# Low-rank experts of a four-layer gated decoder: routing by pairs of tiles, ups written ahead of downs

## The chip, the cores and the metric

The kernel runs on one core of a Trainium2 chip. The engines are named as in the profile: PE (TensorE matmuls, with PEld for its weight loads), DVE (VectorE), ACT (ScalarE), POOL (GpSimd) and SP (SyncE, which issues the DMAs). The metric is the device time of one execution, in microseconds (us).

## What is computed

The reference runs 32 sequences of 64 tokens, each token a row of 128 floats, through four layers. Each layer adds a gated attention and then a gated feed-forward to the rows. The change touches one of the eight pieces, the feed-forward of the third layer: every token picks two of four experts, whose weights are one shared matrix plus a low-rank correction of their own.

```python
x = x + jnp.tanh(g_xattn[2]) * _L2_xattn_ref(_layernorm(x), ctx, ctx, mask, ...)
x = x + jnp.tanh(g_ffn[2]) * _L2_ffn_ref(_layernorm(x, axis=-1), Wg, bg, Wi, Wo, A, B)

def _L2_ffn_ref(x, Wg, bg, Wi, Wo, A, B):        # E = 4 experts, F = 512, D = 128
    logits = jnp.einsum('bsd,ed->bse', x, Wg) + bg
    scores = jax.nn.softmax(logits, axis=-1)
    topv, topi = jax.lax.top_k(scores, TOP_K)     # TOP_K = 2
    w = jnp.sum(jax.nn.one_hot(topi, E) * topv[..., None], axis=-2)
    base = jnp.einsum('bsd,fd->bsf', x, Wi)
    lora = jnp.einsum('bser,efr->bsef', jnp.einsum('bsd,erd->bser', x, A), B)
    h = jax.nn.relu(base[:, :, None, :] + lora)
    expert_out = jnp.einsum('bsef,df->bsed', h, Wo)
    return jnp.einsum('bse,bsed->bsd', w, expert_out)
```

## The kernel before

The 2048 rows are worked in four blocks of 512 rows. A block is four tiles of 128 rows, which lie on the partitions; tiles 0 and 1 are the first pair, tiles 2 and 3 the second. Each block passes eight stages one after the other (`ffn0`, `attention`, `ffn1`, `attention`, `ffn2`, `perceiver`, `attention`, `ffn3`), so a stage runs four times in the kernel. All of it is written by hand: each engine has its own list of instructions, in the order of the code, and waits on semaphores. An engine never passes over an instruction that waits. There is no scheduler, and no data moves by DMA in the stages spoken of here.

The work touched is `ffn2`. The matrix `w_f2e` holds, for each expert, the shared matrix plus its correction, made once at the start. All matmuls are in float32, each recorded as two passes, so four 128x512 matmuls show as eight instructions.

The stage in front of it is an `attention` (turn 3). It ends with a normalisation of the rows on DVE: pair 0 is normalised while its last two tiles are still on their way, pair 1 after them. Each pair takes bn_stats, bn_aggr, a variance, a root that POOL computes (L267), and a scaling (L292) that writes `xn`.

`ffn2` before, engine by engine:

- PE runs `turn_pairs` (L349): three 128x512 matmuls of constants, `keep_clock` (L347), whose results nobody reads, then the transposes of pair 0 and pair 1 (L361). Then come the router for all four tiles (L1254), the four 128x512 ups (L1263) of tile 0 and of tile 1, and from there, per tile, `turn`: four transposes (L1271) of the summed experts and four matmuls (L1278), the down. The next tile's ups follow it.
- ACT copies the transposed rows (L377), takes the exponentials of the routing (L1294) and waits for the routing weights of all tiles, `comb_ready`. Then it runs, per tile and expert, a relu of the ups scaled by the expert's weight (L1303), and per tile a copy of the transposed sum (L1309).
- DVE does the routing of all four tiles: logits (L1321), the best eight (L384), the places of the best two (L387, L388), one-hots (L394 to L396), the softmax's sum and division (L1330 to L1333). Then it adds the four experts of a tile (L1340, L1343, L1345), adds the down to `x` (L1348), and after tiles 1 and 3 normalises a pair for the next stage.
- POOL computes two roots of the next stage's normalisation.

An up needs its bank free (a relu four ups earlier), a `turn` needs the sum, a down the copy. After it comes `perceiver`. Its PE list begins with the transposes of pair 0 (L367), then two 128x512 matmuls each of the keys (L1422), the queries (L1406) and the values (L1415), and the transposes of pair 1. ACT, DVE and POOL work from those.

## Time and profile before

| | us |
|---|---|
| median of three runs | 1601.91 |
| lowest and highest of the three | 1597.54, 1604.3 |
| the profiled execution | 1598.2 |
| its span, from first to last instruction | 1596.4 |
| mean granted TensorE clock of the span | 0.964 of full speed |
| stage `ffn2` in blocks 0, 1 and 2, by windows | 29.7 each |
| stage `ffn2` in block 3 | 31.9 |

The profile is one execution, and its times are counted from the span's start. A row of the timeline is an instruction or a run of like ones: start, duration, engine, line, operation, output and inputs, count, and in brackets how long the engine had been idle before it and what released it. A granted clock of 1.00 is the full 2.4 GHz, 0.50 is 1.2 GHz, and a value between is a window that holds some of each.

### The profile page before, as it was taken

To read this page: it belongs to the slowest core of one execution; us is meant where nothing else is said; L and a number is where in the kernel's file an instruction comes from. 1 tells how busy PE (TensorE), PEld (TensorE's weight loads), DVE (VectorE), ACT (ScalarE), POOL (GpSimd) and SP (SyncE) were. 2 spreads that over 40 slices of the span, in tenths; PEclk is the share of its full clock that TensorE was granted. 3 is DMA by queue.
4 is the path that set the end of the run, shared out by engine and by line. 5 is a ranking of instruction groups with operands and counts; after the bars stand their busy time and mean duration, and the time that the engine had idled before them with its cause. 6 is when DMAs were issued, how large, how long until landed. Compare 5 with 4: busy or idle time off the path is not lost.

```text
span 1596.4 us, 28486 instructions
## 1 busy us (share of the span) xinstructions
PE 1356.1 (85%) x10940; PEld 896.8 (56%) x10940; DVE 1086.4 (68%) x3253; ACT 746.2 (47%) x1406; POOL 362.1 (23%) x302
## 2 busy tenths in 40 slices
PE   4788987897987998798898899889788799888977
PEld 4455744564654664466465575446556467445745
DVE  3456975877656796686764687687755669658774
ACT  0144544763334643575324553467433455257632
POOL 1131310540131220251014031054013212015300
PEclk8799999999999999999899999999999999899999
DMA  9000000000000000000000000000000000000000
GB/s 355 2 1 1 1 1 1 1 1 17 1 7 1 1 1 1 1 1 16 3 1 7 1 1 1 1 1 2 17 1 7 1 1 1 1 1 2 1 1 7
DMA packets 15094, 18.95 MB, mean 12 GB/s; under 512 B 2776, under 2 KB 13672, under 8 KB 14444
## 3 DMA queue, kind: packets, MB, share of 16 engines
q1 hardware_dynamic: 14960, 17.13, 3.1%
q8 instruction: 88, 1.44, 0.4%
q14 instruction: 46, 0.38, 0.1%
HBM read 16.08 MB, written 1.05 MB: 11 GB/s over the span
## 4 chain that ended last, share of the span: by engine, by line
PE 58%; DVE 24%; ACT 7%; issue 6%; POOL 2%; DVEq 0%; POOLq 0%; ACTq 0%
PE bank L1034 7%; PE bank L1045 5%; PE bank L1422 4%; PE bank L1427 4%; PE bank L846 3%; PE bank L1263 3%; DVE work L640 2%; DVE small L646 2%; PE bank L1833 2%; PE bank L1815 2%; PE bank L870 2%; PE bank L1415 2%; DVE small L639 2%; PE bank L1458 2%; PE bank L347 2%
## 5 line engine op out<-in xcount | busy, mean ns | idle before, releaser
L267 POOL TENSOR_TENSOR root<-variance,minus_half 128x2 f32<-128x2 f32 (+1 forms) x72 | 55.3, 768 | 691.5 <-DVE variance L284 421.1
L1087 ACT ACTIVATE work<-bank,w_f 128x512 f32<-128x512 f32 x128 | 88.0, 688 | 90.4 <-PE bank L1034 90.1
L1045 PEld LDWEIGHTS bank<-w_f1d,work 128*128 128x128 f32 x1024 | 119.1, 192 | 13.4 <-issue 13.4
L1045 PE MATMUL bank<-w_f1d,work 128*128 128x129 f32 x1024 | 119.9, 275 | 0.0
L1034 PE MATMUL bank<-xnT,w_f 128*128 128x512 f32 x256 | 118.5, 608 | 0.0
L1596 ACT ACTIVATE work<-work,small 128x128 f32<-128x128 f32 x256 | 78.5, 390 | 84.8 <-DVE small L1723 84.8
L1654 POOL TENSOR_TENSOR small<-small 128x16 f32<-128x16 f32 x32 | 92.9, 2904 | 106.5 <-DVE small L1682 104.9
L639 DVE TENSOR_REDUCE small<-bank 128x8 f32<-128x512 f32 x96 | 65.6, 684 | 32.6 <-PE bank L506 32.6
L1681 DVE TENSOR_REDUCE small<-work 128x16 f32<-128x1024 f32 x48 | 58.4, 1217 | 40.3 <-ACT work L1560 38.7
L521 PE MATMUL bank<-consts,work 128*128 128x128 f32 x384 | 58.9, 291 | 27.9 <-ACT work L605 27.3
L1422 PE MATMUL bank<-w_x,cxT 128*128 128x512 f32 x128 | 62.3, 608 | 21.9 <-DVE work L1695 17.1
L1427 PEld LDWEIGHTS bank<-consts,work 128*128 128x128 f32 x576 | 64.3, 140 | 29.2 <-issue 16.8
L521 PEld LDWEIGHTS bank<-consts,work 128*128 128x128 f32 x384 | 42.3, 145 | 66.5 <-ACT work L605 42.4
L1427 PE MATMUL bank<-consts,work 128*128 128x128 f32 x576 | 74.8, 275 | 5.2 <-DVE work L1695 2.3
L956 DVE TENSOR_TENSOR work<-bank,work 128x256 f32<-128x256 f32 x64 | 27.2, 425 | 76.1 <-POOL work L921 73.8
L1119 POOL TENSOR_TENSOR small<-small,minus_half 128x4 f32<-128x4 f32 x32 | 42.9, 1340 | 150.1 <-DVE small L1173 150.1
L870 PEld LDWEIGHTS bank<-w_l,work 128*128 128x128 f32 x352 | 53.0, 199 | 40.0 <-ACT work L902 31.8
L1034 PEld LDWEIGHTS bank<-xnT,w_f 128*128 128x128 f32 x256 | 47.1, 193 | 48.9 <-issue 48.9
L846 PE MATMUL bank<-w_l,xnT 128*128 128x512 f32 x128 | 73.2, 662 | 0.0
L605 ACT ACTIVATE work<-work 128x512 f32<-128x512 f32 x96 | 59.4, 632 | 28.3 <-DVE work L640 28.2
L612 ACT COPY work<-bank 128x512 f32<-128x512 f32 x96 | 53.0, 585 | 40.0 <-PE bank L521 40.0
L377 ACT COPY xnT<-bank 128x256 f32<-128x256 f32 x32 | 11.2, 374 | 126.1 <-PE bank L361 126.1
(284 smaller groups left out, 3211.5 us busy)
## 6 DMA issues: line engine op xcount, KB each, us to landing
w_f<-in_f_dram SPq DMA_DIRECT2D x1, 2616.0 KB
w_f<-in_f_dram SPq DMA_DIRECT2D x1, 2180.0 KB, 26.5
w_x<-in_x_dram SPq DMA_DIRECT2D x1, 2115.0 KB
w_l<-in_l_dram SPq DMA_DIRECT2D x1, 2088.5 KB, 20.7
w_f1d<-in_f1d_dram SPq DMA_DIRECT2D x4, 512.0 KB
work<-in_x_dram SPq DMA_DIRECT2D x4, 256.0 KB, 2.9
work<-in_ctx_dram SPq DMA_DIRECT2D x4, 256.0 KB, 3.3
out_dram<-x SPq DMA_DIRECT2D x4, 256.0 KB, 2.3
```

Of the source, the lines that this page charges most:

```text
L521: m = pe.transpose(banks[4 + half][:, (c % 4) * P:(c % 4 + 1) * P], p_sb[t % 2][:, c * P:(c + 1) * P], ident)
L605: act.activation(p_sb[t % 2][:, own], s_sb[t % 2][:, own], ACT.Exp).then_inc(p_ready, 1)
L639: link(dve.tensor_reduce(mx[:, t, hs], s, AX, ALU.max))
L846: m = pe.matmul(a[:, :], xt, k_l0["gu"][:, g * 512:(g + 1) * 512], start=True, stop=True)
L870: m = pe.matmul(banks[6 + t % 2][:, 0:D], hidT[s % 2][:, c * P:(c + 1) * P], k_l0["down"][:, (2 * g + c) * D:(2 * g + c + 1) * D], start=( ...
L1034: pe.matmul(banks[n % 3][:, :], k_f1["w1"][:, e * 512 + c * P:e * 512 + (c + 1) * P], xnT[:, :], start=True, stop=True).then_inc(up_done, 1)
L1045: pe.matmul(z_of(e, t)[:, 0:129], hT[e % 2][:, c, t * P:(t + 1) * P], w_f1d[:, c, e, :], start=(c == 0), stop=(c == 3))
L1087: act.activation(hT[e % 2][:, c, :], banks[n % 3][:, :], ACT.Relu, bias=k_f1["b1"][:, n:n + 1]).then_inc(hT_ready, 1)
L1422: pe.matmul(banks[j][:, :], cxT[:, b, :, :], half_of(k_x3["wkv"], j), start=True, stop=True).then_inc(k_done, 1)
L1427: m = pe.transpose(bank[:, (c % 4) * P:(c % 4 + 1) * P], rows[:, c * P:(c + 1) * P], ident)
L1596: ins = act.activation(s_sb[b % 2][:, c * P:(c + 1) * P], s_sb[b % 2][:, c * P:(c + 1) * P], ACT.Exp, bias=negmax[b % 2][:, c:c + 1])
L1654: pool.tensor_tensor(k_rs, k_ssq, half_power, ALU.pow).then_inc(k_rooted, 1)
```

## The change

Only `ffn2` and the table of fill matmuls change.

- The three fill matmuls ahead of the stage's rows go.
- PE transposes pair 0, routes it and computes two ups of tile 0 before it transposes pair 1; the second pair's router stands between the ups of tile 0. The transposes go to banks 4 and 5.
- The routing on DVE is done for two tiles at a time. The first pair's is run whole; the second's is cut in three and laid between the adds of tile 0.
- The relus of tile 0 have the scale 1.0 and don't wait for the routing. DVE multiplies the weights in while it adds: one multiplication (L1378) and three multiply-adds (L1382) take the place of three adds.
- The ups of tile t+2 now stand behind the transposes of tile t and ahead of its down.

```diff
@@ -35,7 +35,7 @@
-FILL_BEFORE_ROWS = (0, 0, 0, 2, 3, 0, 0, 3)
+FILL_BEFORE_ROWS = (0, 0, 0, 2, 0, 0, 0, 3)
@@ -1247,16 +1250,15 @@
-                    turn_pairs(pe, prev, turn_no, xn)
-                    wait_for(pe, prev.all_used)
-                    pe.wait_ge(rowsT_ready, due(rowsT_ready, 2 * turn_no + 2))
...
-                    m.then_inc(routed, 1)
-
-                    def up(t):
...
+                    def route(pair):
+                        pe.wait_ge(rowsT_ready, due(rowsT_ready, 2 * turn_no + pair + 1))
+                        for t in pair_tiles(pair):
+                            m = pe.matmul(banks[6 + pair][:, t * 4:(t + 1) * 4], xnT[:, t * P:(t + 1) * P], k_f2["wg"],
+                                          start=True, stop=True)
+                        m.then_inc(routed, 1)
+
+                    def up(t, experts):
+                        for e in experts:
                             n = 4 * t + e
                             if n >= 4:
                                 pe.wait_ge(r_ready, due(r_ready, n - 3))
...
                             m = pe.transpose(banks[4 + t % 2][:, c * P:(c + 1) * P], r[t % 2][0][:, c * P:(c + 1) * P],
                                              ident)
                         m.then_inc(turned, 1)
+
+                    def down(t):
                         pe.wait_ge(gT_ready, due(gT_ready, t + 1))
+                        pe.wait_ge(comb_ready, due(comb_ready, t % 2 + 1))
...
@@ -1279,34 +1284,56 @@
-                    for t in range(TILES + 1):
-                        if t < TILES:
-                            up(t)
-                        if t == 0:
-                            pe.wait_ge(comb_ready, due(comb_ready, 1))
-                        if t >= 1:
-                            turn(t - 1)
+                    turn_pair(pe, turn_no, xn, 0, banks[4])
+                    wait_for(pe, prev.all_used)
+                    route(0)
+                    up(0, (0, 1))
+                    turn_pair(pe, turn_no, xn, 1, banks[5])
+                    up(0, (2,))
+                    route(1)
+                    up(0, (3,))
+                    up(1, range(4))
+                    for t in range(TILES):
+                        turn(t)
+                        if t + 2 < TILES:
+                            up(t + 2, range(4))
+                        down(t)
 
-                    take_pairs(act, turn_no)
-                    act.wait_ge(shifted, due(shifted, 1))
-                    act.activation(ex, shifted_lg, ACT.Exp).then_inc(exp_ready, 1)
+                    def relus(t, experts):
+                        for e in experts:
+                            act.wait_ge(up_done, due(up_done, 4 * t + e + 1))
+                            if t >= 2 and e == 0:
+                                act.wait_ge(turned, due(turned, t - 1))
+                            weight = 1.0 if t == 0 else comb[:, t, e:e + 1]
+                            act.activation(r[t % 2][e], banks[e][:, :], ACT.Relu, scale=weight).then_inc(r_ready, 1)
+
+                    def exps(pair):
...
+                        own = slice(2 * pair, 2 * pair + 2)
+                        act.wait_ge(shifted, due(shifted, pair + 1))
+                        act.activation(ex[:, own, :], shifted_lg[:, own, :], ACT.Exp).then_inc(exp_ready, 1)
+
+                    def take(t):
...
+                        act.copy(gT[t % 2], banks[4 + t % 2][:, :]).then_inc(gT_ready, 1)
+
+                    take_pair(act, turn_no, 0, banks[4])
+                    relus(0, (0, 1))
+                    take_pair(act, turn_no, 1, banks[5])
+                    exps(0)
+                    relus(0, (2, 3))
                     act.wait_ge(comb_ready, due(comb_ready, 1))
-                    for t in range(TILES + 1):
-                        if t < TILES:
-                            for e in range(4):
-                                act.wait_ge(up_done, due(up_done, 4 * t + e + 1))
-                                if t >= 2 and e == 0:
-                                    act.wait_ge(turned, due(turned, t - 1))
-
-                                act.activation(r[t % 2][e], banks[e][:, :], ACT.Relu,
-                                               scale=comb[:, t, e:e + 1]).then_inc(r_ready, 1)
-                        if t >= 1:
-                            act.wait_ge(turned, due(turned, t))
-                            if t >= 3:
-                                act.wait_ge(down_done, due(down_done, t - 2))
-                            act.copy(gT[(t - 1) % 2], banks[4 + (t - 1) % 2][:, :]).then_inc(gT_ready, 1)
+                    relus(1, (0, 1))
+                    exps(1)
+                    relus(1, (2, 3))
+                    for t in range(TILES):
+                        take(t)
+                        if t + 2 < TILES:
+                            act.wait_ge(comb_ready, due(comb_ready, 2))
+                            relus(t + 2, range(4))
 
@@ -1317,32 +1344,59 @@
-                    dve.wait_ge(routed, due(routed, 1))
...
+
+                    def routing(pair):
+                        own, pw = slice(2 * pair, 2 * pair + 2), [P, 2, 4]
+                        dve.wait_ge(routed, due(routed, pair + 1))
+                        logits = banks[6 + pair][:, 8 * pair:8 * pair + 8].rearrange("p (t e) -> p t e", t=2)
+                        link(dve.tensor_tensor(lg[:, own, 0:4], logits,
+                                               k_f2["bg"].unsqueeze(1).to_broadcast(pw), ALU.add))
+                        link.last_of([dve.max(best[:, t, :], lg[:, t, :]) for t in pair_tiles(pair)])
+                        dve.tensor_tensor(shifted_lg[:, own, :], lg[:, own, 0:4], best[:, own, 0:1].to_broadcast(pw),
                                           ALU.subtract).then_inc(shifted, 1)
-
-                    best, place = top_two(dve, link, lg, 8, 160, with_best=shift)
-                    dve.wait_ge(exp_ready, due(exp_ready, 1))
...
+                        yield
+                        link.last_of([dve.max_index(where[:, t, :], best[:, t, :], lg[:, t, :]) for t in pair_tiles(pair)])
+                        link(dve.tensor_copy(place[:, own, :], where[:, own, 0:2]))
+                        iota = k_const["iota"][:, 0:4].unsqueeze(1).to_broadcast(pw)
+                        link.last_of([dve.tensor_tensor(one, iota, place[:, own, k:k + 1].to_broadcast(pw), ALU.is_equal)
+                                      for k, one in enumerate((comb[:, own, :], tmp[:, own, :]))])
+                        link(dve.tensor_tensor(comb[:, own, :], comb[:, own, :], tmp[:, own, :], ALU.add))
+                        yield
+                        dve.wait_ge(exp_ready, due(exp_ready, pair + 1))
+                        link(dve.tensor_reduce(den[:, own, 0], ex[:, own, :], AX, ALU.add))
+                        link(dve.reciprocal(den[:, own, :], den[:, own, :]))
+                        link(dve.tensor_tensor(ex[:, own, :], ex[:, own, :], den[:, own, :].to_broadcast(pw), ALU.mult))
+                        link(dve.tensor_tensor(comb[:, own, :], comb[:, own, :], ex[:, own, :], ALU.mult))
+                        dve.sem_inc(comb_ready, 1)
+                        yield
+                    def add_experts(t, steps):
+
+                        acc = r[t % 2][0]
+                        dve.wait_ge(r_ready, due(r_ready, 4 * t + 2))
+                        if t == 0:
+                            link(dve.tensor_scalar(acc, acc, comb[:, t, 0:1], None, ALU.mult))
+                        for e in (1, 2, 3):
+                            dve.wait_ge(r_ready, due(r_ready, 4 * t + e + 1))
+                            if t == 0:
+                                ins = dve.scalar_tensor_tensor(acc, r[t % 2][e], comb[:, t, e:e + 1], acc, ALU.mult, ALU.add)
+                            else:
+                                ins = dve.tensor_tensor(acc, acc, r[t % 2][e], ALU.add)
+                            if e == 3:
+                                ins.then_inc(sum_ready, 1)
+                            else:
+                                link(ins)
+                                some(steps, 1)
+
+                    run(routing(0))
+                    second = routing(1)
                     next_rows = iter(())
                     for t in range(TILES + 1):
                         some(next_rows, 3)
                         if t < TILES:
-                            dve.wait_ge(r_ready, due(r_ready, 4 * t + 2))
-                            link(dve.tensor_tensor(r[t % 2][0], r[t % 2][0], r[t % 2][1], ALU.add))
-                            some(next_rows, 1)
-                            dve.wait_ge(r_ready, due(r_ready, 4 * t + 3))
...
+                            add_experts(t, next_rows if t else second)
+                        if t == 0:
+                            run(second)
                         if t >= 1:
```

On PE, from the last project of the attention to the second down, the list before was:

```order
L547 MATMUL bank<-w_x,small 128x128
L347 MATMUL bank<-w_x,consts 128x512 x3
L361 MATMUL bank<-consts,xn 128x128 x4
L1254 MATMUL bank<-w_f,xnT 128x4 x4
L1263 MATMUL bank<-w_f2e,xnT 128x512 x8
L1271 MATMUL bank<-consts,work 128x128 x4
L1278 MATMUL bank<-w_f,work 128x128 x4
L1263 MATMUL bank<-w_f2e,xnT 128x512 x4
L1271 MATMUL bank<-consts,work 128x128 x4
L1278 MATMUL bank<-w_f,work 128x128 x4
```

The same stretch of PE's list now (L1256 is the router, L1265 the ups, L1273 the transposes, L1283 the downs):

```order
L547 MATMUL bank<-w_x,small 128x128
L367 MATMUL bank<-consts,xn 128x128 x2
L1256 MATMUL bank<-w_f,xnT 128x4 x2
L1265 MATMUL bank<-w_f2e,xnT 128x512 x2
L367 MATMUL bank<-consts,xn 128x128 x2
L1265 MATMUL bank<-w_f2e,xnT 128x512
L1256 MATMUL bank<-w_f,xnT 128x4 x2
L1265 MATMUL bank<-w_f2e,xnT 128x512 x5
L1273 MATMUL bank<-consts,work 128x128 x4
L1265 MATMUL bank<-w_f2e,xnT 128x512 x4
L1283 MATMUL bank<-w_f,work 128x128 x4
L1273 MATMUL bank<-consts,work 128x128 x4
```

Three matmuls left the front, four ups moved from behind each of the first two downs to the front of it.

At the end of the stage, PE's list up to the first transposes of the perceiver (L367), before and now:

```order
L1263 MATMUL bank<-w_f2e,xnT 128x512 x4
L1271 MATMUL bank<-consts,work 128x128 x4
L1278 MATMUL bank<-w_f,work 128x128 x4
L1271 MATMUL bank<-consts,work 128x128 x4
L1278 MATMUL bank<-w_f,work 128x128 x4
L367 MATMUL bank<-consts,xn 128x128 x2
```

```order
L1265 MATMUL bank<-w_f2e,xnT 128x512 x4
L1283 MATMUL bank<-w_f,work 128x128 x4
L1273 MATMUL bank<-consts,work 128x128 x4
L1283 MATMUL bank<-w_f,work 128x128 x4
L1273 MATMUL bank<-consts,work 128x128 x4
L1283 MATMUL bank<-w_f,work 128x128 x4
L367 MATMUL bank<-consts,xn 128x128 x2
```

The last four ups now stand ahead of three downs, where they stood ahead of two.

On DVE, from the first routing's end to the first tile's sum, now (the three pieces of the second routing lie between the multiply-adds):

```order
L1369 TENSOR_TENSOR small<-small 128x8
L1378 TENSOR_SCALAR work<-work,small 128x512
L1382 SCALAR_TENSOR_TENSOR work<-work,small 128x512
L1352 TENSOR_TENSOR small<-bank,w_f 128x2x4
L1354 MAX small<-small 128x8 x2
L1355 TENSOR_TENSOR small<-small 128x8
L1382 SCALAR_TENSOR_TENSOR work<-work,small 128x512
L1358 MAX_INDEX small<-small 128x8 x2
L1359 CAST small<-small 128x4
L1361 TENSOR_TENSOR small<-consts,small 128x8 x2
L1363 TENSOR_TENSOR small<-small 128x8
L1382 SCALAR_TENSOR_TENSOR work<-work,small 128x512
```

Before, three adds (L1340, L1343, L1345) stood in this place behind the whole routing.

## Rows read from the trace of the kernel before

**Rows 1.** The page, part 4: shares of the chain that ended last.

```profile
PE 58%; DVE 24%; ACT 7%; issue 6%; POOL 2%; DVEq 0%; POOLq 0%; ACTq 0%
```

**Rows 2.** Chain that ended last, block 0's stage: start, length, what.

```profile
246.79 0.61 DVE xn L292 x2
...
252.36 0.18 DVE small L1333
252.63 0.70 ACT work L1303
253.32 0.14 issue
253.46 3.69 PE bank L1263 x8
```

**Rows 3.** Windows over the stage, blocks 0, 3: width, PE, PEld, DVE, ACT, POOL busy, PEclk.

```profile
243.60:273.30 29.70, 25.00 (x100) 14.00 (x101) 16.28 (x57) 13.43 (x23) 1.39 (x2) 1.00 0.00 0
1392.30:1424.20 31.90, 27.71 (x100) 15.22 (x101) 16.08 (x57) 13.33 (x23) 1.39 (x2) 0.91 0.00 1
```

**Rows 4.** Timeline of block 0, PE in the stage.

```profile
244.09 2.74 PE L347 MATMUL bank<-w_x,consts 128*128 128x512 f32 x6
...
256.97 0.60 PE L1271 MATMUL bank<-consts,work 128*128 128x128 f32 x4
...
258.38 1.16 PE L1278 MATMUL bank<-w_f,work 128*128 128x128 f32 x8 [0.82 <-ACT work L1309]
...
259.38 3.60 PE L1263 MATMUL bank<-w_f2e,xnT 128*128 128x512 f32 x8
...
273.34 0.38 PE L367 MATMUL bank<-consts,xn 128*128 128x128 f32 x2
```

**Rows 5.** Timeline of block 0, DVE at the routing.

```profile
247.58 0.09 DVE L1319 MEMSET small<- 128x32 f32 x1 [0.18 <-DVE xn L292]
...
249.64 0.17 DVE L1321 TENSOR_TENSOR small<-bank,w_f 128x16 f32<-128x16 f32 x1 [1.97 <-PE bank L1254]
249.85 0.37 DVE L384 MAX8 small<-small 128x8 f32<-128x8 f32 x4
...
250.35 0.09 DVE L387 MATCH_VALUE_LOAD small<-small 128x8 f32 x1
...
251.02 0.17 DVE L388 CAST small<-small 128x8 f32<-128x8 uint32 x1
```

**Rows 6.** Groups by line and form, DVE: busy and mean ns of one.

```profile
L1189 DVE SCALAR_TENSOR_TENSOR x<-work,small,x 128x128 f32<-128x128 f32 x128 | 36.8, 347 | 1.2 <-DVE small L1186 0.2
...
L1170 DVE TENSOR_SCALAR work<-work 128x512 f32<-128x512 f32 x32 | 13.7, 427 | 1.1
...
L1340 DVE TENSOR_TENSOR work<-work 128x512 f32<-128x512 f32 x16 | 11.1, 692 | 18.7 <-ACT work L1303 18.7
...
L762 DVE SCALAR_TENSOR_TENSOR work<-bank,tg,xn_next 128x512 f32<-128x512 f32 x4 | 3.0, 745 | 0.0
```

**Rows 7.** Timeline of block 0, DVE and POOL at the stage's end.

```profile
265.43 0.35 DVE L1348 SCALAR_TENSOR_TENSOR x<-bank,tg,x 128x128 f32<-128x128 f32 x1 [0.93 <-PE bank L1278]
...
266.62 0.17 DVE L282 TENSOR_SCALAR variance<-norm_small 128x2 f32<-128x2 f32 x1
266.86 0.70 POOL L267 TENSOR_TENSOR root<-variance,minus_half 128x2 f32<-128x2 f32 x1 [20.11 <-DVE variance L282]
```

**Rows 8.** Timeline, PE, at gaps of other stages.

```profile
384.13 0.76 PE L521 MATMUL bank<-consts,work 128*128 128x128 f32 x4 [2.40 <-ACT work L605]
...
1535.04 1.12 PE L521 MATMUL bank<-consts,work 128*128 128x128 f32 x4 [2.40 <-ACT work L605]
```

**Rows 9.** Windows around falls of the clock; columns as in Rows 3.

```profile
384.00:388.00 4.00, 3.30 (x56) 2.58 (x56) 3.28 (x6) 2.58 (x6) 0.00 (x0) 0.57 0.01 2
1534.00:1542.00 8.00, 6.75 (x69) 3.99 (x70) 6.11 (x10) 3.37 (x6) 0.00 (x0) 0.57 0.01 3
1391.00:1399.00 8.00, 6.43 (x12) 2.99 (x12) 3.96 (x14) 0.38 (x2) 1.14 (x2) 0.57 0.00 0
```

**Rows 10.** Timeline, PE at half clock, blocks 3 and 0.

```profile
1392.95 5.33 PE L347 MATMUL bank<-w_x,consts 128*128 128x512 f32 x6
...
385.45 1.11 PE L521 MATMUL bank<-consts,work 128*128 128x128 f32 x4 [0.56 <-ACT work L605]
```

**Rows 11.** Chain that ended last, block 0, into the perceiver.

```profile
274.93 1.96 PE bank L1422 x4
276.88 0.87 PE bank L1406 x2
277.78 0.60 ACT work L1569
```

25 lines of the change are left out of this document (7 added, 18 removed).

## The prediction

> **What bounds the kernel now.** I read the shares of the chain first: PE holds 58% of it and DVE 24% [rows 1], so what counts in a stage is who hands work to PE. Then the same chain inside the changed stage [rows 2]. It runs from the second pair's normalised rows (246.79, ready at 247.40) over transposes, router and the whole routing on DVE to the first relu at 252.63, and only that relu frees the bank for the next ups at 253.46. From there the stage is a loop of transposes, copy, down and four ups. The windows say how long the stage is: 29.7 us in block 0 and alike in blocks 1 and 2, 31.9 us in block 3, where the granted clock was 0.91 [rows 3]. The stage is 7.6% of the span, so even a tenth of it is 12 us in four blocks.
>
> The profiled execution took 1598.2 us, 1.8 us more than its span. I make the sum against it and carry the difference over to the median of 1601.9, which lies 3.7 us higher.
>
> **Head of the stage: from the second pair's rows to the first tile's transposes.** Before, the transposes L1271 began at 256.97 [rows 4], 9.57 us after the rows at 247.40. In the new order PE works ahead on pair 0 (rows ready at 244.3): its transposes, two routers and two ups end at about 247.6, the six other ups, the second pair's transposes and routers at 253.7, with 0.86 us an up (3.60 us for four and a bit of overlap [rows 4]). ACT follows each up by about a microsecond. DVE becomes what decides, since it can't start to route before the second pair is normalised. Its list, start to start:
> - memset and first routing. For four tiles the routing took 2.88 us from 249.64 to the end of L1333 at 252.53 [rows 2, 5]. With two tiles the four MAX8 (0.37) halve, and the four searches (250.35 to 251.02, 0.67) halve; the other ten steps read so few elements that they keep their time. That gives 2.88 - 0.19 - 0.33, some 2.4, plus 0.13 for the memset from 247.58: ready at 250.2.
> - the multiplication L1378, 128x512 with one scalar per partition. The trace has it with constants, 427 ns [rows 6]; with a scalar that is read I take 0.48, bounds 0.43 and 0.75. With its semaphore 0.52.
> - three multiply-adds L1382: 745 ns each for the same shape [rows 6], 0.78 with the semaphore, 2.34. The adds that they replace took 692.
> - the first two pieces of the second routing, which lie between them: 0.6 and 1.1, the parts of the 2.4 above.
> 250.2 + 0.52 + 2.34 + 1.7 is 254.8, so the transposes start at 254.85, 2.1 us earlier. PE is done with its ups at 253.7 and has 1.2 us of slack there; ACT, with the last relu of tile 0 at about 251.1, has more. The removed fills cost nothing before in blocks 0 to 2: they ran from 244.09 to 246.83 [rows 4], and pair 1 was ready only at 247.40.
>
> **Middle and end: from the first transposes to the perceiver.** Before: 256.97 to 273.34, 16.37 us [rows 4]. Now transposes 0.5, ups 3.44, down 0.96, transposes 0.5, ups 3.44: the second down starts at 263.7, and PE never waits, since the copy (0.6) and the sums lie under the ups. That part is the gain of ups in front of downs, some 0.9 us for each copy that PE waited for. But DVE takes the second down into x only 1.2 us after it starts (258.38 to 259.58 before), at 264.9, and nothing of its list may pass that. Behind it stand the next normalisation's first steps (265.43 to 266.8 before, 1.4 us [rows 7]), an add of 0.72, the two scalings at 0.6, and two adds: the last tile's sum is ready at 269.2. PE has nothing to do from the end of the third down at 266.9 until then, a gap of 2.35 us. Last transposes 269.3, copy 0.64, down 270.6, and the perceiver's transposes start at 271.6: 16.7 us, 0.3 longer than before. What the new order won in the middle, DVE's order takes back at the end.
>
> Net with the clock held: 2.1 - 0.3 = 1.8 us a block, for PE's and DVE's ends alike, **-7.1 us** in four blocks.
>
> **Block 3.** There the clock fell ahead of the stage and the three fills took 5.33 us [rows 10] where they take 2.74; pair 1's transposes came 2.3 us later than its rows allowed. Without fills that is gone, and the ups at half clock stay inside the slack of 1.2 us and DVE's list. **-2.3 us.**
>
> **The clock at the end of the stage.** PE's clock was 1.00 through the whole stage in three blocks [rows 3]. The new gap of 2.35 us stands behind transposes and a down, and is followed by 0.6 us of transposes, another 0.67 us of waiting, a down and 1.2 us for the perceiver's first copy. The nearest rows are the gaps of 2.40 us ahead of L521 in the third attention [rows 8]: there are four, one a block (384.13, 765.83, 1148.13, 1535.04), and the clock fell at each of them, between 0.2 us before the gap's end and 1.0 us after it. It then stood at half for 3.4 us (three of the four; a 4 us window at 0.57) or for 6.9 us (8 us windows at 0.57 [rows 9]), as it did at 1391, where PE had little to do in the fall's first half. I expect the fall here in all four blocks. Its price: a 128x512 pass costs 0.43 us more at half clock (5.33 against 2.74 for six [rows 10]), and four 128x128 transposes 0.5 more (1.11 [rows 10] against 0.60 [rows 4]). The perceiver's start is on the chain [rows 11]: eight passes of keys and queries and four of values, from 273.1. A spell of 6.9 us that begins between 268 and 271.5 reaches 275 to 278, so it takes in two to five and a half of these passes, 0.9 to 2.4 us, and some part of the last transposes and down, 0 to 1.3 us. I take 2.1; the bounds are 0.5 (a short spell) and 3.6. **+8.4 us**, 2.0 to 14.4.
>
> The Trainium skill speaks against the change here: TensorE: Matmul & The Clock Gate, Part 4: PE-mode transpose, says that transposes don't count as PE being busy in the way that matmuls do, and two of the three things that PE does between 264.7 and 273 are transposes. By that rule the fall would be sure in all four blocks; the trace can't separate it, since the gaps of rows 8 fell without it.
>
> **Sum:** -7.1 - 2.3 + 8.4 = -1.0: 1597.2 us for the profiled execution, **1600.9 us** against the median. With the bounds of the fall alone, 1594.5 to 1607.
>
> **Rivals.**
> - The clock holds at the end, or falls so late that it is back before the perceiver's matmuls. For it speaks that the head of the stage has gaps of 1.4 us with little between them and fell in one block of four. Against it, the four falls out of four at 2.40 us. Then -9.4: 1592.5 us.
> - Slower: the fills were what held the clock at the head. If they go, PE does only short work from 238 to 245.8 and the clock falls there in all blocks, for 6.9 us as at 1391 [rows 9]. The ups from 245.8 to 252.3 then pass at half, 7.5 passes instead of 15: 3.2 us lost, less PE's slack of 1.2, 2.0 a block, on top of the fall at the end. It decides from the third block on. 1600.9 + 8 = 1609 us, 1611 with the far bound of the spell. Against it: at 1391 the clock fell in spite of the fills to come.
> - The change doesn't do what it says: DVE's list is as long as before. With L1378 at 0.75, and halves of the routing that take as long as the whole, the first transposes come 0.9 us earlier, not 2.1, and the sum is +4: 1605 us.
> - Multiply-adds from SBUF at half rate. The rows speak against it: L1189 with both tensors in SBUF takes 347 ns [rows 6], L1348 with one in PSUM 0.35 us [rows 7]. From 128 to 512 columns the time grows by 0.40, so a doubled stream costs 0.53 more each, 1.6 a block, 6.4 in all: 1607 us. This is what the Trainium skill would have, Vector Engine (DVE) Microarchitecture Reference, 7. Points that are easy to get wrong: this instruction with two SBUF sources that aren't bf16 runs at half throughput. The trace does not agree.
>
> **Chances.** Clock falls at the end, about no change: 0.50. Clock holds: 0.27. Falls at the head too: 0.10. DVE's list no shorter: 0.08. Multiply-adds at half rate: 0.05. About 0.5%, 8 us, is what a measurement of this kernel can tell from no change, so faster is under 1593.9 and slower over 1609.9. The held clock lies at the first edge and gives most of faster, with a small part of the forecast's: 0.28. Slower: the head's fall and the far ends of two others: 0.14. Same: 0.58. The range goes from 1591, under which lies a quarter of the held clock's case, to 1607, over which lie the head's fall and some of the last two.
>
> **What the new profile would show.** The first transposes of the stage (L1273) some 7.5 us after pair 1's rows, where it was 9.6; the perceiver's transposes 16.7 us behind them; a gap of PE of about 2.35 us ahead of the last L1273, released by DVE's last add; a granted clock under 0.9 in the windows of the perceiver's first 5 us in three or four blocks, and 1.00 at the ups. L1382 at 745 ns and L1378 at 480. Wrong would be a clock of 1.00 through the perceiver's start, ups at half clock, or a first sum that waits for ACT's relus.

## The result and the profile after

| | before | after |
|---|---|---|
| median, us (runs) | 1600.07 (4) | 1617.24 (4) |
| range, us | 1597.54 to 1604.3 | 1615.41 to 1621.38 |
| profiled execution, us | 1598.2 | 1615.41 |
| its span, us | 1596.4 | 1613.6 |
| mean granted clock | 0.964 | 0.940 |

The changed kernel takes 1.0102 of the time before, interval 1.0081 to 1.0123: 16 us slower. The forecast was no change, and 1617 lies ten microseconds over its range.

The chain's shares are those of [rows 1], but for a point of ACT. The page's own strip (before, then after) of the granted clock, 40 slices in tenths, already says where to look: it is under 9 in ten slices, where before's is in four, and the mean over the span fell by 0.024.

```profile
PEclk8799999999999999999899999999999999899999
...
PEclk8799987999999999899999998889999999989989
...
PE 58%; DVE 24%; issue 6%; ACT 6%; POOL 2%; DVEq 0%; POOLq 0%; ACTq 0%
```

I cut each block in three at instructions that both kernels have: the **head**, from the last L547 of the attention to the first transposes of the stage; the **tail**, from there to the perceiver's first transposes L367; and the **start** of the perceiver, to its second L367. Microseconds, blocks 0 to 3, from the timelines of the two:

| | before | after |
|---|---|---|
| head | 13.21, 13.21, 13.21, 15.50 | 12.97, 11.02, 12.98, 11.01 |
| tail | 16.37, 16.37, 16.38, 16.38 | 18.29 in all four |
| start | 6.82 in all four | 9.03, 8.87, 9.06, 8.90 |

Heads are 7.2 us less in sum, tails 7.7 more, starts 8.6 more. The two profiles are single executions, and they part before the change does anything: block 0's last L547 stands at 243.76 before and at 245.20 after, since the clock had fallen at other places in the two by then. So 1.4 us of the 17.2 between the spans aren't the change's.

PE's timeline of the kernel after, tail of block 0 (start, length, line, what; in brackets the wait and its releaser), answers [rows 4]:

```profile
267.76 0.60 PE L1273 MATMUL bank<-consts,work 128*128 128x128 f32 x4
269.03 1.16 PE L1283 MATMUL bank<-w_f,work 128*128 128x128 f32 x8 [0.68 <-ACT work L1321]
272.80 1.12 PE L1273 MATMUL bank<-consts,work 128*128 128x128 f32 x4 [2.61 <-DVE work L1384]
274.59 2.08 PE L1283 MATMUL bank<-w_f,work 128*128 128x128 f32 x8 [0.68 <-ACT work L1321]
276.46 0.63 PE L367 MATMUL bank<-consts,xn 128*128 128x128 f32 x2
278.30 3.75 PE L1476 MATMUL bank<-w_x,cxT 128*128 128x512 f32 x4 [1.20 <-ACT cxT L1606]
```

The gap of 2.61 us is there, released by DVE's last add. Everything behind it takes twice its time: transposes 1.12 for 0.60, a down 2.08 for 1.16, and the perceiver's four passes 3.75 where [rows 11] has 1.96. The windows show the clock (width, busy of PE, PEld, DVE, ACT, POOL, granted clock, DMA), block 0 ahead of, in and behind the spell (a stretch at half clock), then blocks 1 to 3 in it:

```profile
268.00:272.00 4.00, 1.51 (x12) 1.08 (x10) 3.11 (x10) 0.58 (x1) 1.08 (x1) 1.00 0.00 0
272.00:282.00 10.00, 7.32 (x19) 4.49 (x20) 2.81 (x10) 2.20 (x4) 0.69 (x1) 0.50 0.00 0
282.00:286.00 4.00, 3.87 (x11) 1.59 (x9) 2.64 (x4) 2.74 (x6) 0.00 (x0) 0.97 0.00 0
657.00:668.00 11.00, 7.29 (x19) 4.46 (x20) 3.71 (x12) 2.20 (x4) 0.69 (x1) 0.53 0.00 0
1046.80:1057.00 10.20, 7.56 (x19) 4.67 (x20) 2.81 (x10) 2.35 (x5) 0.69 (x1) 0.50 0.00 0
1432.40:1442.80 10.40, 7.31 (x19) 4.47 (x20) 3.13 (x11) 2.20 (x4) 0.69 (x1) 0.51 0.00 0
```

The clock fell in all four blocks, as forecast, from 2.4 to 1.2 GHz; in block 0 it fell inside the gap, at 272.0, and came back at 282.3, after 10.2 us, where I had taken 6.9. The releaser of the gap is DVE's list, block 0, which answers [rows 7]:

```profile
267.96 0.35 DVE L1402 SCALAR_TENSOR_TENSOR x<-bank,tg,x 128x128 f32<-128x128 f32 x1 [2.37 <-PE bank L1283]
268.34 0.49 DVE L275 BATCH_NORM_STATS2 bn_small<-x 128x6 f32<-128x128 f32 x2
...
269.39 1.08 POOL L267 TENSOR_TENSOR root<-variance,minus_half 128x2 f32<-128x2 f32 x1 [21.21 <-DVE variance L282]
270.58 0.60 DVE L292 TENSOR_SCALAR xn<-x,norm_small,root 128x128 f32<-128x128 f32 x2 [0.66 <-POOL root L267]
271.21 1.53 DVE L1384 TENSOR_TENSOR work<-work 128x512 f32<-128x512 f32 x2
```

DVE takes x, normalises, and only then makes the two adds that PE waits for. POOL's root, beside an add of DVE, took 1.08 us; in [rows 7] it takes 0.70.

**The head.** The heads come in two kinds, 11.0 and 13.0. Windows of the ups in block 0 (long; block 2 reads the same) and block 1 (short), and block 0 around the fall:

```profile
245.00:252.00 7.00, 6.25 (x15) 3.53 (x16) 4.28 (x25) 1.32 (x3) 0.69 (x1) 0.53 0.00 1
633.00:644.00 11.00, 9.28 (x30) 4.36 (x30) 8.96 (x45) 5.98 (x12) 0.69 (x1) 1.00 0.01 1
244.20:244.70 0.50, 0.00 (x0) 0.00 (x0) 0.50 (x1) 0.00 (x0) 0.07 (x1) 1.00 0.00 0
244.70:245.20 0.50, 0.00 (x1) 0.01 (x1) 0.47 (x3) 0.00 (x0) 0.00 (x0) 0.52 0.00 0
```

```profile
245.20 0.80 PE L547 MATMUL bank<-w_x,small 128*128 128x128 f32 x2 [1.40 <-DVE small L647]
```

The long heads are those in which the clock fell before the ups. It fell at 244.7, half a microsecond ahead of the last L547, which already takes 0.80 us for the 0.49 that it takes at full clock; in block 2 it fell at 1019.5, ahead of the L547 at 1019.96. The removed fills would have stood behind this L547, so they could not have held the clock in these two heads. In the short one of block 1, PE's and DVE's steps answer the sum of the prediction: the second pair's rows are ready at 636.80 and the first transposes start 7.40 us later, and PE has waited 1.11 us for DVE's last multiply-add.

```profile
636.20 0.60 DVE L292 TENSOR_SCALAR xn<-x,norm_small,root 128x128 f32<-128x128 f32 x2 [0.81 <-POOL root L267]
...
639.66 0.48 DVE L1378 TENSOR_SCALAR work<-work,small 128x512 f32<-128x512 f32 x1
...
644.20 0.65 PE L1273 MATMUL bank<-consts,work 128*128 128x128 f32 x4 [1.11 <-DVE work L1382]
```

### The profile page after: what moved, and what is told of

It is laid out like the page before. It is cut to its first block, busy times and chain, and to the rows that moved or that the text cites. A ratio compares the mean times of both kernels' runs of the same rounds, so it can differ in the third digit from the quotient of the medians.

```text
span 1613.6 us, 28506 instructions
## 1 busy us (share of the span) xinstructions
PE 1374.0 (85%) x10916; PEld 912.1 (57%) x10916; DVE 1093.3 (68%) x3297; ACT 746.9 (46%) x1410; POOL 363.3 (23%) x302
## 4 chain that ended last, share of the span: by engine, by line
PE 58%; DVE 24%; issue 6%; ACT 6%; POOL 2%; DVEq 0%; POOLq 0%; ACTq 0%
PE bank L1034 7%; PE bank L1045 5%; PE bank L1476 4%; PE bank L1481 4%; PE bank L846 3%; PE bank L347 2%; PE bank L1265 2%; DVE work L640 2%; DVE small L646 2%; PE bank L1887 2%; PE bank L1869 2%; PE bank L870 2%; PE bank L1469 2%; DVE small L639 2%; PE bank L1512 2%
## 5 line engine op out<-in xcount | busy, mean ns | idle before, releaser
L267 POOL TENSOR_TENSOR root<-variance,minus_half 128x2 f32<-128x2 f32 (+1 forms) x72 | 56.7, 788 | 698.4 <-DVE variance L284 427.9
L1476 PE MATMUL bank<-w_x,cxT 128*128 128x512 f32 x128 | 69.5, 668 | 21.9 <-DVE work L1749 17.1
L640 DVE TENSOR_TENSOR work<-bank,small 128x512 f32<-128x512 f32 x96 | 66.4, 691 | 3.3
```

The source lines that it names most:

```text
L640: ins = dve.tensor_tensor(d, s, mx[:, t, hs].unsqueeze(2).to_broadcast([P, 8, SEQ]), ALU.subtract)
L1476: pe.matmul(banks[j][:, :], cxT[:, b, :, :], half_of(k_x3["wkv"], j), start=True, stop=True).then_inc(k_done, 1)
```

## The experiments

**Theory A:** the gap of 2.6 us ahead of the last transposes lets the clock fall, and this alone costs more than the head wins; what is left is a gain. **Rival B:** the new order is slow in itself (DVE's longer list, relus from SBUF, two routings), and the clock is a side effect. **Rival C:** what is lost is lost because everything behind moved in time, so that the clock falls at other places; any shift would do the same. A further question was what the removed fills had been worth.

The results, each against the kernel before on the same chip; heads, tails and starts in us for blocks 0 to 3 as above:

| run | ratio (interval) | head | tail | start |
|---|---|---|---|---|
| e1_fill_tail_gap | 0.9986 (0.9969, 1.0002) | 12.99, 12.81, 12.98, 11.03 | 16.90, 16.96 x3 | 6.82 x4 |
| e3_downs_first | 0.9957 (0.9936, 0.9979) | 11.03, 12.98 x3 | 16.29 to 16.37 | 6.81 x4 |
| e4_ups_first_alone | 1.0079 (1.0053, 1.0105) | 13.20 x3, 14.04 | 17.65, 17.64, 17.65, 17.23 | 9.94, 10.06, 8.59, 9.07 |
| e2_before_no_head_fills | 1.0053 (1.0034, 1.0073) | 15.83, 15.97, 16.19, 15.21 | 16.38 x4 | 6.82 x4 |
| e6_sum_before_norm | 0.9881 (0.9846, 0.9916) | 11.02, 11.03, 12.92, 12.93 | 14.75 to 14.82 | 6.85, 8.54, 6.84, 6.85 |
| e7_downs_first_attention_fill | 0.9941 (0.9921, 0.9960) | 11.03 x4 | 17.98, 16.30, 17.98, 16.29 | 6.82 x4 |
| e10_exps_ahead | 0.9971 (0.9955, 0.9986) | 11.02, 12.98, 12.91, 12.84 | 16.3 to 16.4 | 6.81 x4 |
| e8_sum_first_and_fill | 0.9930 (0.9909, 0.9952) | 11.04, 11.38, 11.03, 11.84 | 14.82 x4 | 6.85 x4 |
| e5_before_shifted | 1.0061 (1.0041, 1.0081) | 13.34, 14.03, 13.21, 14.26 | 16.38 x4 | 6.82 x2, 8.51, 6.82 |
| e12_before_shifted_less | 1.0048 (1.0029, 1.0068) | 15.50, 13.20 x3 | 16.38 x4 | 6.82, 6.81, 8.51, 6.81 |
| e11_after_shifted | 1.0153 (1.0132, 1.0174) | 12.80, 11.02, 11.03, 12.94 | 18.29 x3, 17.77 | 8.90, 8.94, 8.80, 8.58 |
| e13_after_shifted_less | 1.0146 (1.0118, 1.0174) | 12.82, 11.03, 12.93, 12.99 | 18.28, 18.29, 17.77, 17.76 | 8.93, 8.80, 8.58, 8.62 |

### The gap filled

The kernel after with four passes on PE (whose result nobody reads) ahead of the last transposes:

```diff
                     for t in range(TILES):
+                        if t == TILES - 1:
+                            pe.wait_ge(r_ready, due(r_ready, 14))
+                            keep_clock(pe, banks[1], 2)
                         turn(t)
```

> The changed kernel with two matmuls of constants (four passes, about 1.7 us) ahead of the last tile's transposes, where PE waits 2.6 us for DVE. Theory A, the gap lets the clock fall: the clock stays at 1.00, the last transposes to the perceiver take 16.7 us instead of 18.3 from the first ones, the perceiver's start 6.8 instead of 8.9, and some more behind it comes back too, 4 to 5 us a block in all: 1597 to 1602 us against 1617 of the changed kernel. Theory B, the fall has nothing to do with the gap (missing fills at the head, or the transposes): the clock still falls and the time stays at 1614 to 1620.

Median 1600.83 us. PE's timeline of this kernel, block 0, and the windows over tail and start of the four blocks:

```profile
267.64 1.88 PE L347 MATMUL bank<-w_x,consts 128*128 128x512 f32 x4
...
270.42 0.66 PE L1273 MATMUL bank<-consts,work 128*128 128x128 f32 x4 [0.89 <-DVE work L1387]
```

```profile
266.00:283.00 17.00, 12.38 (x44) 6.29 (x44) 10.61 (x35) 7.04 (x13) 4.08 (x6) 1.00 0.00 0
651.00:668.00 17.00, 12.48 (x44) 6.28 (x44) 10.26 (x34) 6.91 (x14) 4.41 (x6) 1.00 0.00 0
1036.00:1053.00 17.00, 12.35 (x46) 6.28 (x44) 10.58 (x36) 7.03 (x13) 3.94 (x6) 1.00 0.00 0
1419.00:1436.00 17.00, 12.48 (x44) 6.28 (x44) 10.61 (x34) 6.92 (x14) 4.36 (x6) 1.00 0.00 0
```

DVE's list and all waits for it are as they were; only the clock differs, 1.00 in all four blocks. Tails fall from 18.29 to 16.96 and starts from 8.97 to 6.82: 14 us in four blocks, of the 1.16% (18 us) that the two ratios differ by. That is theory A's; B can't explain it. The gain that A promised besides is hardly there (the interval reaches 1), since here the clock fell at the head in three blocks. The other 4 us lie outside of tail and start and aren't shown to be the gap's.

### Downs before ups, and ups before downs alone

The kernel after, with the down back in front of the ups of the next tile but one:

```diff
                         turn(t)
+                        down(t)
                         if t + 2 < TILES:
                             up(t + 2, range(4))
-                        down(t)
```

> The changed kernel with the downs ahead of the ups again, as before; head, routing by pairs and relus stay changed. Theory A: last gap gone, tail 16.4 us and perceiver's start 6.8, the head keeps its 2.2 us where the clock is held there: 1596 to 1602 us. Theory B: no more than the 0.3 us a block that the order itself costs comes back: 1614 to 1619 us.

Median 1593.72 us. PE's timeline of this kernel, block 0: the last transposes wait for nobody, and the window over tail and start stands at 1.00 (as it does in the other three blocks).

```profile
266.77 0.60 PE L1273 MATMUL bank<-consts,work 128*128 128x128 f32 x4
268.18 1.16 PE L1283 MATMUL bank<-w_f,work 128*128 128x128 f32 x8 [0.82 <-ACT work L1321]
269.18 0.60 PE L1273 MATMUL bank<-consts,work 128*128 128x128 f32 x4
```

```profile
265.00:282.00 17.00, 12.91 (x49) 6.71 (x47) 10.22 (x30) 9.29 (x18) 3.98 (x6) 1.00 0.00 0
```

With everything else of the change kept, this is 0.4% under before (a difference of the size that a mere shift can make, as shown below), and the tail is no longer than before's. So what made the change slower is one edit of the five, ups in front of downs. The reverse puts that edit alone into the kernel before:

```diff
-                    for t in range(TILES + 1):
-                        if t < TILES:
-                            up(t)
-                        if t == 0:
-                            pe.wait_ge(comb_ready, due(comb_ready, 1))
-                        if t >= 1:
-                            turn(t - 1)
+                    up(0)
+                    pe.wait_ge(comb_ready, due(comb_ready, 1))
+                    up(1)
+                    for t in range(TILES):
+                        turn(t)
+                        if t + 2 < TILES:
+                            up(t + 2)
+                        down(t)
```

> The kernel before with only the ups put ahead of the downs; fills, routing and relus as before. Theory A: the clock falls at the end of the stage in all four blocks, 1.9 us in the tail, 2.2 in the perceiver's start and about 1 behind it: 1616 to 1621 us. Theory B (the head is the cause): 1599 to 1603 us.

Median 1615.24 us. Its timeline, block 0, and the windows over tail and start, blocks 0 and 3 (in block 1 the spell is as long as in block 0, in block 2 as in block 3):

```profile
273.44 0.66 PE L1271 MATMUL bank<-consts,work 128*128 128x128 f32 x4 [2.49 <-DVE work L1348]
```

```profile
270.00:287.00 17.00, 12.59 (x36) 6.84 (x35) 7.44 (x19) 4.95 (x10) 1.76 (x2) 0.70 0.00 0
...
1432.00:1449.00 17.00, 11.51 (x36) 6.34 (x36) 8.37 (x24) 5.89 (x12) 1.76 (x2) 0.80 0.00 0
```

The same gap (2.49 us), the same four falls, 0.8% lost: this edit alone is enough. Adding it and removing it point to the same cause from both sides.

### The sum before the normalisation

If DVE's order makes the gap, DVE's order can close it. The kernel after, where the sum of a tile is finished before any step of the next normalisation:

```diff
                     for t in range(TILES + 1):
-                        some(next_rows, 3)
                         if t < TILES:
-                            add_experts(t, next_rows if t else second)
+                            add_experts(t, iter(()) if t else second)
                         if t == 0:
                             run(second)
+                        run(next_rows)
```

> The changed kernel with one thing moved on DVE: the last tile's three adds come ahead of the next stage's normalisation steps instead of behind and between them. PE's order stays ups first. Theory A: the last gap shrinks from 2.6 to about 0.6 us, so the clock holds and the tail takes 15 us instead of 18.3 and the perceiver's start 6.8 instead of 8.9: 1588 to 1597 us. Theory B (ups first costs in itself, whatever the gap): 1608 us or more.

Median 1583.39 us against 1601.11: 0.9881, under the range that was expected. DVE, POOL and PE of this kernel, block 0:

```profile
267.65 2.15 DVE L1384 TENSOR_TENSOR work<-work 128x512 f32<-128x512 f32 x3
...
269.86 0.66 PE L1273 MATMUL bank<-consts,work 128*128 128x128 f32 x4 [0.36 <-DVE work L1384]
...
270.76 0.70 POOL L267 TENSOR_TENSOR root<-variance,minus_half 128x2 f32<-128x2 f32 x1 [21.32 <-DVE variance L282]
...
272.30 0.41 PE L367 MATMUL bank<-consts,xn 128*128 128x128 f32 x2
```

The gap goes from 2.61 to 0.36 us, the normalisation is still done before PE wants it at 272.30, and the tail is 14.8 us, 1.6 less than before. The gain of ups in front of downs, which the prediction put at some 0.9 us for each copy and saw taken back by DVE, is real once DVE's order lets it through. This kernel is faster than the one before and the changed one.

### The head: what the fills were worth

The kernel before with its three fills at the head taken out, one number:

```diff
-FILL_BEFORE_ROWS = (0, 0, 0, 2, 3, 0, 0, 3)
+FILL_BEFORE_ROWS = (0, 0, 0, 2, 0, 0, 0, 3)
```

> The kernel before without the three matmuls of constants ahead of the stage, nothing else. Theory A: they matter only at the head; the block that lost 2.3 us through slow fills gains it, another may lose up to 3 us by ups at half clock: 1597 to 1606 us. Theory B, the missing fills are what costs the 17 us: 1612 us or more.

Median 1611.41 against 1602.82: it lies between the two ranges. That is 8.6 us, and the longer heads of the profiled execution make up 8.1 of them. PE's timeline of this kernel, block 0, and the window at its head:

```profile
244.49 0.49 PE L547 MATMUL bank<-w_x,small 128*128 128x128 f32 x2 [1.40 <-DVE small L647]
...
248.23 0.69 PE L361 MATMUL bank<-consts,xn 128*128 128x128 f32 x2 [2.62 <-DVEq L307]
...
251.18 9.31 PE L1263 MATMUL bank<-w_f2e,xnT 128*128 128x512 f32 x16
```

```profile
244.00:251.00 7.00, 3.17 (x14) 2.34 (x14) 3.11 (x14) 0.74 (x2) 0.69 (x1) 0.60 0.00 0
```

The fills that I had costed at nothing held the clock in this order of PE: without them it falls at 245.4, where they would have run, and the heads of blocks 0 to 2 grow by 2.6 to 3.0 us. In block 3, where it fell ahead of the last L547 with the fills and without, the head shrinks by 0.3.

So there are two kinds of falls at a head, and only one of them is the fills'. I read where each began, by windows, in all traces without the attention's fill that comes next. With the three fills (before, e4, e5, e12) the clock fell in 5 heads of 16, each time 0.4 to 0.9 us ahead of the last L547 and never behind it. Without them (after, e1, e2, e3, e6, e10, e11, e13) it fell in 22 of 32: in 8 ahead of it as before, in 14 some 0.9 to 1.6 us behind it, where fills would have run. Both falls in the profile of the kernel after are of the first kind.

Would the head be short in all blocks if PE had some work in the attention's end? The kernel with downs first, and two passes more there:

```diff
+                        if turn_no == 3 and step == TILES + 2:
+                            wait_for(pe, (s_ready, 6))
+                            keep_clock(pe, banks[1], 1)
                         if 0 <= step - 3 < TILES:
...
                         turn(t)
+                        down(t)
                         if t + 2 < TILES:
                             up(t + 2, range(4))
-                        down(t)
```

> The kernel with the changed head and the downs first, and one matmul of constants (two passes) put into PE's wait ahead of the last project of the attention in front of the stage, where PE idles 1.4 us. Theory A for the head: it holds the clock there, so the stretch from the last project to the first transposes takes 11.0 us in all four blocks, where it took 13.0 in three: 6 us less than the same without the fill, 1585 to 1592 us. Rival: one fill is too little or the fall comes from elsewhere: no change, 1592 to 1597.

All four heads are 11.03, so the heads can be held. But the ratio, 0.9941, can't be told from that of downs first alone. In the profiled execution the clock now fell in the middle of the stage in blocks 0 and 2 (from 259 and from 1024 on; eight passes of the ups took 5.21 us instead of 3.60), and the tails there took 17.98: there the fall was moved, not removed. That execution was the slowest of the six (1596.3 us; the others 1589.6 to 1593.3), so the others may have had fewer falls.

A rival for the long heads was ACT's order: in a fallen head its first exp stands behind a relu whose up is late, and DVE waits for it.

```profile
252.40 0.22 ACT L1315 ACTIVATE small<-small 128x8 f32<-128x8 f32 x1
...
252.73 0.16 DVE L1366 TENSOR_REDUCE small<-small 128x2 f32<-128x8 f32 x1 [2.00 <-ACT small L1315]
```

This is the kernel after, block 0. The experiment keeps downs first, and puts the exp behind the first relu:

```diff
                     take_pair(act, turn_no, 0, banks[4])
-                    relus(0, (0, 1))
-                    take_pair(act, turn_no, 1, banks[5])
+                    relus(0, (0,))
                     exps(0)
+                    relus(0, (1,))
+                    take_pair(act, turn_no, 1, banks[5])
```

> The kernel with the changed head and the downs first, with the first pair's exponentials put ahead of tile 0's second relu on ACT. In blocks whose head runs at half clock the exponentials waited 2.0 us behind that relu and the second pair's copy, and DVE's routing with them. Theory: those heads take about 11.5 us instead of 13.0; the others 11.0 to 11.3: 1588 to 1593 us. Rival (the half clock costs the 2 us through the ups themselves): the heads stay at 13.0, 1593 to 1596.

The median was 1596.57 us, over both ranges, and the idea fell: fallen heads are 12.84 to 12.98 as they were. In block 1 of this kernel the exp now comes at once, at 627.54, and the transposes follow straight on PE's own ups.

```profile
627.54 0.20 ACT L1315 ACTIVATE small<-small 128x8 f32<-128x8 f32 x1
...
631.20 4.54 PE L1265 MATMUL bank<-w_f2e,xnT 128*128 128x512 f32 x10
...
635.57 0.60 PE L1273 MATMUL bank<-consts,work 128*128 128x128 f32 x4
```

So the 2 us of a fallen head come from PE's passes at half clock themselves, and another order on ACT doesn't help.

Both good edits together, the attention's fill (as in the diff above) and the sum before the normalisation:

> The changed kernel with the last tile's adds ahead of the normalisation and with the matmul of constants in the attention's last wait. Both gaps are then short or filled. Theory A: heads of 11.0 us in all four blocks (two were 12.9 without the fill), tails of 14.8, perceiver's start 6.8: 3.9 us better in the two heads and 1.7 in one start than without the fill, 1576 to 1584 us. Rival (what is won at the head is lost to falls elsewhere): 1583 or more.

Median 1585.83, 0.9930 against 0.9881 without the fill. Tails and starts came as the theory had them, 14.82 and 6.85, and so did two of the heads; in the other two (11.38 and 11.84) the clock fell later, 2.5 to 3.0 us behind the last L547. Yet the whole is no faster: heads, tails and starts together are 4.2 us less than without the fill, the profiled span is 1.5 us more, so what the stage gained was lost outside of it. By the times the rival holds.

### Does any shift do it?

Extra copies of the logits on DVE, in block 0's routing of another stage only, move everything behind by about 1.9 us (8 copies in place of one) or 0.9 us (4). The kernel before with 8 and 4, the kernel after with 8 and 4:

```diff
-                    link(dve.tensor_copy(logits, banks[6][:, 0:68].rearrange("p (t e) -> p t e", t=TILES)))
+                    for _ in range(8 if i == 0 else 1):
+                        link(dve.tensor_copy(logits, banks[6][:, 0:68].rearrange("p (t e) -> p t e", t=TILES)))
```

> The kernel before with one small copy of the first block's first router repeated seven more times (about 1.9 us on DVE, once), which moves everything behind it later and changes nothing else. It measures what a mere shift does through the falls of the clock in all stages. Theory A (the 17 us are the gap's): the shift costs its 1.9 us and a few us either way, 1598 to 1607 us. Theory C (the falls elsewhere are dealt anew by any shift, and that is most of the 17 us): a change of 8 us or more.

> The kernel before with a one-time delay of about 0.9 us. With the 1.9 us one, it gives how far the time goes with the position alone: the longer delay cost 9 us. Theory A: between 1597 and 1611 us, tails of 16.4 and starts of 6.8 in all blocks, differences only in heads and in other stages. Theory C: a tail or start of this stage changes too.

> The changed kernel with the one-time delay of about 1.9 us in the first block's router. Theory A (the gap lets the clock fall wherever it stands): tails of 18.3 and starts of 8.6 to 10 us in all four blocks again, 1612 to 1625 us. Theory C (the 17 us were an unlucky position of the falls): one or more of the four tails holds its clock, or the time falls to 1608 or less.

> The changed kernel with the one-time delay of about 0.9 us. Theory A: tails of 18.3 us and starts of 8.6 to 10 in all four blocks, 1610 to 1624 us. Theory C: 1608 us or less.

| | unshifted | by 0.9 us | by 1.9 us |
|---|---|---|---|
| before | 1 | 1.0048 | 1.0061 |
| after | 1.0102 | 1.0146 | 1.0153 |

Rival C is half right. A shift of one or two microseconds costs both kernels 0.4 to 0.6%, 7 to 10 us, several times its own length, and a fall of the clock at a start (8.51) or a head (15.50) appears where there was none. But at each of the three positions the change costs the same, 0.9 to 1.0%, and in the stretch from the first transposes of the attention ahead of the stage to those of the attention behind the perceiver, the four blocks take 12.9, 9.7 and 10.5 us more after than before (617.8 and 630.7; 624.5 and 634.2; 622.1 and 632.6). So the 1% is the change's own. The shifts are less exact than their names: already ahead of the copies, where the delay hasn't happened, the executions stand up to 2.5 us apart (block 0's first router L835 begins between 61.40 and 63.90), and block 0's last L547 stands at 243.8, 247.1 and 245.9 in the three of before. They are three positions, not steps of 0.9. What the three runs of the kernel after share, and none of before has, are tails of 17.8 to 18.3 and starts of 8.6 to 9.1 in all four blocks.

## Why the prediction was wrong, by its steps

- **Head, clock held.** Right. 7.40 us from rows to transposes in block 1, forecast 7.45; L1378 485 ns for 480 taken; L1382 751 for 745. The 1.2 us of slack on PE was 1.11. The kernel after, all instructions of the two lines (min, median, max in ns):

```profile
L1382 DVE SCALAR_TENSOR_TENSOR work<-work,small x12: 743/751/751, 254.2 to 1418.2; 128x512 f32<-128x512 f32 x12
...
L1378 DVE TENSOR_SCALAR work<-work,small x4: 485/485/485, 253.6 to 1414.4; 128x512 f32<-128x512 f32 x4
```

- **Multiply-adds at half rate.** Refused: 751 ns with both tensors in SBUF, 745 with one in PSUM [rows 6]. The Trainium skill's rule (Vector Engine (DVE) Microarchitecture Reference, 7. Points that are easy to get wrong) does not hold for this instruction here.
- **Tail, clock held.** Nearly right: 16.7 forecast, 16.9 to 17.0 in the run with the gap filled. The gap was 2.61, not 2.35 us. DVE waited 0.66 us for POOL's root, which took 0.38 us longer beside the add; that is more than the whole difference.
- **Block 3.** The number is right, by luck: forecast 2.1 and 2.3 less at the head, measured 4.5 (15.50 to 11.01). But the forecast had the clock fall there again and the slow ups stay inside the slack. It didn't fall there. Where it did fall ahead of the head, in blocks 0 and 2, the head took 2.0 us more than the 11.0 (12.97), so the slack doesn't hold the slow ups.
- **Clock falls at the end, in all four blocks.** Right, and its mechanism stands by four runs (e1, e3, e4, e6). That transposes don't count as work, which the Trainium skill says (TensorE: Matmul & The Clock Gate, Part 4: PE-mode transpose), none of them separates.
- **Its price. This is the step that failed.** Forecast 2.1 us a block, bounds 0.5 and 3.6. Measured: 1.6 in the tail (18.29 for the 16.7 forecast, gap included) and 2.2 at the perceiver's start (8.97 for 6.82), 3.7 together. The mis-sized part is the length of the spell: it lasted 10.2 us, not 6.9, from 272.0 to 282.3 in block 0. So it took the last transposes and the down from their beginning and four and a half of the perceiver's passes besides, where I had weighed these two as one or the other. The shifted runs of the kernel after hold the test: in blocks 2 and 3 of e13 the spell behind the same gap of 2.61 us lasted 6.8 us. There the tail took 17.77 and the start 8.58 to 8.62, which is 0.8 and 1.8 over the run with the gap filled, 2.6 in all; the spells of 10.2 us cost 1.3 and 2.2 by the same measure, 3.5. Below are the spell of e13's block 2, and a stretch of 10 us at half clock at the start of the kernel before, which was there to be read. I had taken the two lengths that the rows showed as all that there were.

```profile
1048.30:1055.10 6.80, 5.55 (x14) 3.61 (x15) 1.86 (x8) 1.62 (x3) 0.69 (x1) 0.50 0.00 0
```

```profile
23.00:33.00 10.00, 4.33 (x19) 3.94 (x20) 3.18 (x12) 0.78 (x1) 0.01 (x1) 0.50 0.99 423
```

- **A fall at the perceiver's end, which the prediction doesn't have.** From the perceiver's start to the end of the next attention's first transposes the kernel after takes another 1.3 us a block. A window of it, block 0, has 0.79 (the other three blocks have the same), where the same work of before stood at 1.00. That this is the gap's doing too is not shown, and two runs speak against it: with the gap filled and the tail at full clock (e1) the clock fell at the same place in three blocks of four, and with the gap there but no other edit (e4) it did not in blocks 0 and 1. What makes it fall there stays open. The kernel after, block 0, and e1, block 2:

```profile
371.00:379.00 8.00, 5.72 (x34) 4.65 (x34) 2.53 (x12) 1.61 (x4) 0.69 (x1) 0.79 0.00 0
```

```profile
1135.50:1143.50 8.00, 5.96 (x38) 4.88 (x40) 2.68 (x11) 1.86 (x4) 0.69 (x1) 0.79 0.00 0
```

- **Fills cost nothing and hold nothing.** Wrong as a rule: e2 shows them holding the clock in three blocks, and of the heads without them 14 of 32 fell where they would have run. But in the profile of the kernel after they cost nothing by their absence. Both of its falls began half a microsecond ahead of the last L547, and in block 0 nothing that the change touches had run by then. The rival "slower: the clock falls at the head" had the price right, 2.0 us a block, but it gave the fills as the cause and all four blocks. These 3.9 us are a matter of where the falls landed, as before's own fall at 1391 was.

The terms together, for two spans that differ by 17.2 us: -9.4 as forecast with the clock held, +6.3 tail, +8.6 start, +5.3 rest of the perceiver, +3.9 heads, -1.5 the attention in front of the stage in block 3 (where before's clock fell), and +4.3 in other stages, 1.4 of it ahead of the change: 17.5. Of the miss, the tail and the start are the step that failed: 14.9 for the 8.4 that I had. Put right, they take the forecast from 1600.9 to 1607.4, just over the edge of its range. The other 12 us lie where the sum has no term: heads, the perceiver's end, other stages. I can't put them down to single causes; the shifted runs show that several microseconds of that kind come with any shift.

## What to carry to other kernels

Ahead of PE work that is on the chain, a new wait such as the 2.5 and 2.6 us here is not priced by its own length: look at what PE does behind it, and count twice the time of all of that for as long as the longest spell in the whole trace, the kernel's start included. Before giving work to an engine in another order, look for the two instructions that another engine waits for and put them ahead of what is only due later; the same edit was worth +0.8% and, with DVE's order right, some of -1.2%. And a fill that "costs nothing because PE would wait anyway" may be there for the clock; take it out in a run of its own before counting on its going. When the clock falls near an edit, look first whether it fell ahead of the first instruction that the edit touches; if it did, the edit is not its cause there.

## What the runs showed of the hardware

- The granted clock fell in all four blocks at a gap of 2.61 us (in block 0 0.8 us before its end) and of 2.49 (0.6 us behind its end), and in none of four at the same stretch with four passes of matmul in it, 1.88 us, and a gap of 0.89 left. Four passes a block made the kernel some 18 us of 1617 faster, 14 of them in the tails and starts.
- A spell at half clock behind one and the same gap of 2.61 us lasted 10.2 us in some blocks and 6.8 in others (e13), and cost 3.5 and 2.6 us in the stage's tail and the perceiver's start.
- The clock fell at the head in 5 of 16 blocks with three fills and in 22 of 32 without; all 5 began ahead of the place of the fills.
- A delay of 0.9 us in one place cost 0.4 to 0.5% of the whole, in both kernels, and the clock fell at other places. Differences of half a per cent between two orders of this kernel need such a control before a cause is named.
- POOL's L267 on 128x2 took 1.08 us in all four blocks of the kernel after while DVE made one add of two 128x512 tensors, and 0.70 in [rows 7] and in e6, where no such add ran beside it.
- The multiply by a scalar that is read per partition took 485 ns for 128x512, with constants 427 [rows 6].
